# Attention on one NeuronCore: the row maxima are split into high and low part on 128 partitions and turned by VectorE in squares of 32, instead of by a TensorE matmul

## What is computed

```python
q = (x @ wq_w + wq_b).reshape(bs, sl, Q_H, HEAD_DIM)
k = (x @ wk_w + wk_b).reshape(bs, sl, KV_H, HEAD_DIM)
v = (x @ wv_w + wv_b).reshape(bs, sl, KV_H, HEAD_DIM)
qg = q.reshape(bs, sl, KV_H, FACTOR, HEAD_DIM)
scale = 1.0 / jnp.sqrt(jnp.asarray(HEAD_DIM, x.dtype))
attn = jnp.einsum('bqhfd,bkhd->bhfqk', qg, k) * scale
att = jax.nn.softmax(attn, axis=-1)
a = jnp.einsum('bhfqk,bkhd->bqhfd', att, v)
```

## Time and profile before

| | |
|---|---|
| median of three runs | 2863.34 us (2861.27 to 2865.27) |
| profiled execution | 2858.41 us, its span 2856.6 us |
| mean granted TensorE clock | 0.991 |
| TensorE busy | 2765.9 us |
| VectorE busy | 2196.1 us |
| GpSimd busy | 1914.0 us |
| ScalarE busy | 1519.8 us |

### The profile page before, as it was taken

The page is one execution under the profiler, slowest core; times in us unless marked ns, Lnnn a source line. Parts: engine busy times, 40 slices in busy tenths (PEclk is TensorE's granted clock), DMA queues, the critical chain, the costliest instruction groups (busy, mean ns, idle before and its releaser), DMA issues. The chain is left out here.

```text
span 2856.6 us, 48739 instructions
## 1 busy us (share of the span) xinstructions
PE 2765.9 (97%) x14654; PEld 1698.3 (59%) x14654; DVE 2196.1 (77%) x2775; ACT 1519.8 (53%) x2907; POOL 1914.0 (67%) x712
## 2 busy tenths in 40 slices
PE   7999999999999999999999999999999969999997
PEld 4788888874444444444444444444444427888886
DVE  4433343358999999999999999999999968666666
ACT  3111111117766666666666666667666733455444
POOL 2433333318999999999999999999999965111110
PEclk9999999999999999999999999999999989999998
DMA  7544444524444443343444334344433333333331
GB/s 268 178 141 140 140 136 143 151 91 123 95 96 89 87 99 83 86 98 85 90 94 95 89 86 94 89 89 90 99 86 85 71 108 114 111 102 97 111 110 67
DMA packets 167583, 307.60 MB, mean 108 GB/s; under 512 B 50000, under 2 KB 91408, under 8 KB 159376
## 3 DMA queue, kind: packets, MB, share of 16 engines
q1 hardware_dynamic: 158368, 240.05, 28.8%
q0 software_dynamic: 9072, 66.06, 11.3%
HBM read 159.12 MB, written 79.82 MB: 84 GB/s over the span
## 5 line engine op out<-in xcount | busy, mean ns | idle before, releaser
L1022 ACT ACTIVATE p_t<-st_ps 128x512 f32<-128x512 f32 x2048 | 1113.3, 596 | 465.2 <-PE st_ps L1140 393.4
L1040 DVE TENSOR_REDUCE mx<-s_ps 128x1 f32<-128x1024 f32 x1002 | 1172.9, 1209 | 109.3 <-PE s_ps L1114 100.0
L971 POOL TENSOR_TENSOR p_sum<-p_sum,p_t 128x2048 f32<-128x2048 f32 x254 | 1168.6, 4601 | 42.7 <-ACT p_t L1022 26.3
L1140 PE MATMUL st_ps<-q_st,k_st 98*128 98x512 f32 x2048 | 816.9, 438 | 21.4 <-ACT p_t L1022 19.0
L1140 PEld LDWEIGHTS st_ps<-q_st,k_st 98*128 98x128 f32 x2048 | 345.3, 187 | 615.8 <-ACT p_t L1022 515.5
L1114 PE MATMUL s_ps<-k_st,q_st 96*128 96x512 f32 x2004 | 629.9, 395 | 1.5 <-DVE mx L1040 1.3
L1154 PE MATMUL num_ps<-p_t,v_sb 128*32 128x512 f32 x4096 | 546.7, 606 | 0.9 <-ACT p_t L1022 0.9
L1114 PEld LDWEIGHTS s_ps<-k_st,q_st 96*128 96x128 f32 x2004 | 378.8, 189 | 73.4 <-DVE mx L1040 5.4
L1055 DVE TENSOR_REDUCE two_sum<-p_t 128x512 f32<-128x1024 f32 x256 | 317.4, 1241 | 3.1 <-DMA p_sum<-two_sum 3.1
L497 POOL TENSOR_TENSOR o_lo<-side,o_hi 128x512 fp32r<-128x512 f32 x80 | 104.2, 1303 | 321.3 <-ACT o_hi L467 321.1
L971 POOL TENSOR_TENSOR p_sum<-p_t 128x2048 f32<-128x2048 f32 x64 | 312.9, 4889 | 8.6 <-ACT p_t L1022 8.6
(11 more groups left out here) (141 smaller groups left out, 2884.8 us busy)
## 6 DMA issues: line engine op xcount, KB each, us to landing
p_sum<-two_sum POOLq DMA_DIRECT2D x63, 1024.0 KB, 7.0
q_st<-q_hi_d SPq DMA_DIRECT2D x128, 256.0 KB, 4.3
stage<-w_mod SPq DMA_DIRECT2D x48, 512.0 KB, 6.3
q_hi_d<-o_hi SPq DMA_DIRECT2D x64, 256.0 KB, 2.0
q_lo_d<-o_lo SPq DMA_DIRECT2D x64, 256.0 KB, 2.0
q_st<-q_lo_d SPq DMA_DIRECT2D x64, 256.0 KB, 4.1
att_d<-a_sb SPq DMA_DIRECT2D x128, 128.0 KB, 2.3
a_f<-att_d SPq DMA_DIRECT2D x32, 512.0 KB, 4.7
```

Of the source, the lines that this page charges most:

```text
L971: nc.gpsimd.tensor_tensor(total, before, p_t[:, kt, :, :], ALU.add).then_inc(sum_done, 1)
L1022: nc.scalar.activation(p_t[:, s, c, :], st_ps[:, c % 2, :], ACT.Exp, scale=SCALE)\
L1040: nc.vector.tensor_reduce(mx[:, slot % 2, e:e + 1], s_ps[:, e % 2, :], AX_X, ALU.max)\
L1140: nc.tensor.matmul(st_ps[:, c % 2, :], k_st[:, slot // 2, s * P:(s + 1) * P], q_st[:, slot, jj, h * QW:(h + 1) * QW], start=True, stop=True)\
```

## The change

The turn leaves TensorE. ScalarE now negates and rounds `mx` as it is, 128x16 from SBUF, into the left half of `m_parts`, and it does so behind the last exponential of step 4 (`NEGATE_STEP`). VectorE forms the rest into the right half at the beginning of step 5. Behind the `two_sum` of that step it turns `m_parts` in four squares of 32x32 (`m_t`) and copies the result into `m_rows`, which rounds it to fp32r. Each group of 32 partitions of `m_rows` then holds, for 32 queries of each of the 16 tiles, a row of 128 bytes for each part and tile, and SP places it by four transfers instead of two (`put_row`). `den_ps` no longer holds `m_ps`, so `add_sum` waits for `den_taken` alone, and `maximum` and `max_hi` keep their waits on `m_turned`, which VectorE now signals. The same is done once at the end of `project` for pair 0.

```diff
+def put_row(sp, q_st, slot, m_rows, landed):
+    rows = q_st[96:98, slot, :, :].bitcast(F32).rearrange("h j (t b r) -> h b (j t) r", b=4, r=32)
+    for b in range(4):
+        sp.dma_start(rows[:, b, :, :], m_rows[32 * b:32 * b + 32, :].bitcast(F32)).then_inc(landed, 16)
...
-    TURN_STEP = 5
+    NEGATE_STEP = 4
...
-        m_ps = den_ps[0:NS, 0:P]
...
                 def put_max(pair, slot):
-                    sp.wait_ge(m_lo_done, pair + 1)
-                    for n, part in enumerate((m_hi, m_lo)):
-                        sp.dma_start(q_st[STACK + n:STACK + n + 1, slot, :, :].bitcast(F32)
-                                     .rearrange("o j s -> o (j s)"), part[:, :].bitcast(F32))\
-                          .then_inc(m_in, 16)
+                    sp.wait_ge(m_ready, pair + 1)
+                    put_row(sp, q_st, slot, m_rows, m_in)
...
-                def max_hi(pair):
-                    act.wait_ge(m_turned, pair + 1)
-                    if not is_int(pair, 0):
-                        act.wait_ge(m_in, pair * 32)
-                    nc.scalar.activation(m_hi[:, :], m_ps, ACT.Copy, scale=-1.0).then_inc(m_hi_done, 1)
+                def max_hi(pair, slot):
+                    act.wait_ge(max_done, pair * NS + NS)
+                    act.wait_ge(m_turned, pair)
+                    nc.scalar.activation(m_parts[:, 0:NS], mx[:, slot % 2, :], ACT.Copy, scale=-1.0)\
+                      .then_inc(m_hi_done, 1)
...
-                            if c == 1 and s == TURN_STEP and not is_int(pair, NPAIR - 1):
-                                max_hi(pair + 1)
+                            if c == REP - 1 and s == NEGATE_STEP and not is_int(pair, NPAIR - 1):
+                                max_hi(pair + 1, (slot + 1) % QR)
...
-                def max_lo(pair):
+                def max_lo(pair, slot):
                     dve.wait_ge(m_hi_done, pair + 1)
-                    if not is_int(pair, 0):
-                        dve.wait_ge(m_in, pair * 32)
-                    nc.vector.scalar_tensor_tensor(m_lo[:, :], m_ps, -1.0, m_hi[:, :].bitcast(F32), ALU.mult,
-                                                   ALU.subtract).then_inc(m_lo_done, 1)
+                    nc.vector.scalar_tensor_tensor(m_parts[:, NS:2 * NS], mx[:, slot % 2, :], -1.0,
+                                                   m_parts[:, 0:NS].bitcast(F32), ALU.mult, ALU.subtract)\
+                      .then_inc(m_lo_done, 1)
+
+                def turn_max(pair):
+                    dve.wait_ge(m_lo_done, pair + 1)
+                    nc.vector.transpose(m_t[:, :], m_parts[:, :].bitcast(F32)).then_inc(m_turned, 1)
+                    dve.wait_ge(m_turned, pair + 1)
+                    dve.wait_ge(m_in, pair * 64)
+                    nc.vector.tensor_copy(m_rows[:, :], m_t[:, :]).then_inc(m_ready, 1)
...
-                        if s == TURN_STEP + 1 and not is_int(pair, NPAIR - 1):
-                            max_lo(pair + 1)
+                        if s == NEGATE_STEP + 1 and not is_int(pair, NPAIR - 1):
+                            max_lo(pair + 1, (slot + 1) % QR)
                         if s == 0 and not below(pair, 1):
                             add_two(pair - 1, REP - 1)
                         if s in TWO_STEPS:
                             add_two(pair, TWO_STEPS.index(s))
+                        if s == NEGATE_STEP + 1 and not is_int(pair, NPAIR - 1):
+                            turn_max(pair + 1)
...
-                    nc.tensor.matmul(m_ps, mx[:, slot % 2, :], ident[:, :], start=True, stop=True)\
-                      .then_inc(m_turned, 1)
...
-                        pe.wait_ge(m_in, pair * 32 + 32)
+                        pe.wait_ge(m_in, pair * 64 + 64)
...
-                        if is_int(pair, NPAIR - 2):
-                            pe.wait_ge(den_taken, NPAIR - 2)
-                        else:
-                            pe.wait_ge(m_lo_done, pair + 3)
+                        if not below(pair, 1):
+                            pe.wait_ge(den_taken, pair)
```

More of the change, by code:

```diff
@@ L31 @@
     mx: Any
-    m_hi: Any
-    m_lo: Any
+    m_parts: Any
+    m_t: Any
+    m_rows: Any
     s_ps: Any
@@ L39 @@
     m_turned: Any
+    m_ready: Any
     m_hi_done: Any
@@ L396, in do @@
                         elif ev[0] == "negate":
-                            sp.wait_ge(ahead.m_lo_done, 1)
-                            for n, part in enumerate((ahead.m_hi, ahead.m_lo)):
-                                sp.dma_start(ahead.q_st[3 * HD + n:3 * HD + n + 1, 0, :, :].bitcast(F32)
-                                             .rearrange("o j s -> o (j s)"), part[:, :].bitcast(F32))\
-                                  .then_inc(ahead.m_in, 16)
+                            sp.wait_ge(ahead.m_ready, 1)
+                            put_row(sp, ahead.q_st, 0, ahead.m_rows, ahead.m_in)
                         elif ev[0] == "rows":
@@ L817, in sem @@
             return ctx.enter_context(nc.semaphore(name))
-        q_st, k_st, mx, m_hi, m_lo, s_ps = ahead.q_st, ahead.k_st, ahead.mx, ahead.m_hi, ahead.m_lo, ahead.s_ps
+        q_st, k_st, mx, s_ps = ahead.q_st, ahead.k_st, ahead.mx, ahead.s_ps
+        m_parts, m_t, m_rows, m_ready = ahead.m_parts, ahead.m_t, ahead.m_rows, ahead.m_ready
         v_sb = sb("v_sb", [P, 2, NKT, HD], F32)
@@ L1199, in do @@
                             add_sum(pair - 1, (slot - 1) % 2)
-                        if s == TURN_STEP and not is_int(pair, NPAIR - 1):
-                            turn_max(pair + 1, (slot + 1) % QR)
                         scores(pair, slot, s, 2)
```

40 lines of the change are left out of this document (17 added, 23 removed).

## The result

The changed kernel takes 3283.48 us, the median of four runs (3280.34 to 3285.73); the kernel before took 2863.89 us beside it. The ratio is 1.1466, with a 95% interval from 1.1451 to 1.1481: 14.7% slower. The forecast was 3234 us, and its range ended at 3280, so the time lies 3.5 us outside the range. The profiled execution has a span of 3278.5 us, and the mean granted clock of TensorE is 0.929 against 0.991 before.

The account below looks back on a forecast made before the run. It took GpSimd to be as full as TensorE, both nearly unbroken. Per pair -0.20 + 4.68 (stall) + 1.5 (clock) = +5.98 us; 62 pairs add 371 to 2858.4, giving 3229, plus 4.9: 3234 us, range 3080 to 3280.

Parts of the forecast that it names:

- The race and the port: Step 5: VectorE's copy comes 0.1 to 0.2 us after a 4.6 us GpSimd sum begins, held to its end.
- The price of the hold: Step 6: TensorE waits for maxima delayed by VectorE's held copy, a stall of 4.68 us a pair.
- rival (a): Attention loop: VectorE's copy is held but TensorE's clock costs nothing; +4.48 us a pair, 3141 us; chance 11%.
- The clock: TensorE after the stall, step 7: 3.4 us at half clock, taken as 1.5 us a pair, bounds 0 to 1.7.
- the forecast alone: Main case, held copy plus low clock: 3165 us (clock 0.6 a pair) to 3270 (clock 1.7, hold 0.3 longer); chance 68%.
- The rest of the change: Attention loop: ScalarE's negating copy, SP's four transfers and the waits cost zero; the turn off TensorE saves 0.20 us a pair.
- GpSimd's ring: GpSimd's work from one join to the next in the attention loop, 25.97 us a pair, idle only 0.66.
- The net 0.23 us of VectorE: Steps 5 and 6: three new VectorE operations issue in 0.42 us, less 0.19 for the dropped `m_lo`.
- rival (c): Step 5: copy unheld, but VectorE's extra work and a held remainder cost 0 to +0.3 us a pair; 2863-2882 us; 7%.
- (b): Attention loop: copy held in only part of the pairs; half of them gives about 3050 us; chance 6%.
- (d): Step 5: copy goes before GpSimd's sum; not slower, 2860 us, or 2850 if GpSimd gave way; chance 8%.

Follow-up runs that it names:

- the run with the clock kept up: Changed kernel plus 16 unread matmuls on TensorE ahead of the first half entry of step 6, inside its wait: 3140.15 us, ratio 1.0973.
- the kernel of two reduces: Changed kernel with both VectorE's copy into `m_rows` and the remainder (`mx` less its rounded part) written as reduces: 2881.78 us, ratio 1.0069.

## Why the prediction came out as it did

**The race and the port: right.** The earlier trace rows gave GpSimd's sum at T5 + 1.70 and the sum of VectorE's steps the copy at T5 + 1.89; the rows after show + 1.78 and + 1.99. The copy was held to the end of the sum in all 62 pairs in which the prediction counted it. That it is the kind of instruction was only argued from the earlier trace rows; the reduce in its place, with 186 ns, shows it. That the GpSimd instruction sets the length is shown by three lengths: 4.37 us from its beginning, 2.38 from its middle, 2.2 with half a sum. The kernel with the copy ahead of the sum shows that the order of issue decides, as the prediction had it. The runs show which instructions exclude each other, and no run shows that a port is the reason. The Trainium skill ("SBUF — State Buffer", section "Who interferes with whom") names casts in a two-port mode and operations with two SBUF inputs on one side, reduces and ScalarE on the other; all four agree here (4365 and 1130 ns held, 186 and 218 not).

**The price of the hold: right.** 4.68 less 0.20 of turn makes 4.48 us a pair; the run with the clock kept up has 4.48 from the medians and 4.49 from the pairs. Its time, 3140 us, is what rival (a) gave with 3141. The parts fit too: the third half entry of step 6 was put at T5 + 8.82 and starts there at + 8.73 (1522.98 against 1514.25), and the numerators ahead of T5 take 1.00 us instead of 1.19 once the turn is gone (1509.68 to 1510.68 in the changed kernel). One detail was missing: the first half entry waits as well, for the first of the two held maxima, and TensorE's long idle time stands ahead of it, with little left ahead of the third. That cost an experiment and not the sum.

**The clock: the step that failed.** The sum had 1.5 us a pair, from 3.4 us at half clock behind one gap of the trace of before, and called 1.7 its upper bound. Measured are 2.31. The surplus of 0.81 us in 62 pairs is 50 us, which is the whole difference between 3234 and 3283.5. In its place stands: the low stretch lasts 6.8 us in most pairs, twice what that gap showed. Over the whole execution, (1 - 0.929) x 2 x 3278.5 = 466 us ran at the low clock against (1 - 0.991) x 2 x 2856.6 = 51 before, 6.7 us a pair. Half of that would be 3.35 us, and 2.31 were lost; part of the low time is idle (1.75 us in the pair shown above, next to none in the following one), and where the rest of the difference went no run shows. One gap was made a bound; the range ended at 3280 for that reason. The trace of before held more. It has a gap of 7.52 us with a low stretch of 6.8 us (0.30 us of the window 2323, six whole ones, 0.54 of the window 2330), and in the attention loop itself an idle time of 0.99 us with 3.4 us at 0.50 behind it:

```profile
2327.60 1.94 PE L1171 MATMUL den_ps<-p_sum,ones 128*32 128x512 f32 x8 [7.52 <-DVE den_t L1064]
...
1058.49 0.99 PE L1140 MATMUL st_ps<-q_st,k_st 98*128 98x512 f32 x2 [0.99 <-ACT p_t L1022]
```

```profile
2324.00:2325.00 1.00, 0.00 (x0) 0.00 (x0) 1.00 (x2) 0.00 (x0) 0.00 (x0) 0.50 0.00 0
...
1061.00:1062.00 1.00, 1.00 (x8) 0.13 (x8) 1.00 (x2) 0.63 (x2) 1.00 (x1) 0.50 0.24 49
```

The prediction's spread for the forecast alone was added up wrongly as well: by its own terms 2863.3 + 62 x (4.48 + 0.6) gives 3178 and not 3165, and a clock of 1.7 with a hold longer by 0.3 gives 3265 and not 3270. Neither would have taken in the result.

**The rest of the change: right.** Turn, negation, transfers, bank and waits were put at nothing beside GpSimd's ring, and the kernel without the copy is at 1.0006. ScalarE's copy, the transfers and the waits need no correction. The net 0.23 us of VectorE was hidden by the hold; where nothing is held, remainder and turn cost nothing (pairs of 25.96) and the third operation 0.27 a pair. That the kernel of two reduces measures 2881.78 us, the upper end of rival (c) with 2882, is luck in part: (c) counted a held remainder, and that kernel has none.

**The rivals.** (b) didn't occur: the copy came 0.18 to 0.31 us behind the sum's start in each pair, where GpSimd had waited for ScalarE and was thereby tied to T5. (d) was right that GpSimd's ring keeps the 0.20 us of TensorE from showing: with nothing held the pair stays at 25.96.

Not settled: why the remainder was kept out for 6.87 us through the ends of two GpSimd instructions in one pair; and what decides whether the clock falls behind an idle time of about 1 us, and whether its low stretch lasts 3.4 or 6.8 us. No run was made for either.

## What to carry to other kernels

Before a small VectorE copy, cast or two-input operation in SBUF is put into a stretch in which GpSimd works without a break, look which GpSimd instruction will be running when it is issued: its remaining length was the length of the hold in all pairs but one here, for an operation of 0.17 or 0.18 us. Write the small operation as a reduce, give it to ScalarE, or drop it, as here where the values were already rounded. To issue it just ahead of the long instruction is not safe: the copy ahead of the sum was still too late in five pairs of 63. And where a stall of TensorE recurs in a loop, count it with the low clock behind it, with the cost that runs show, and look at every low stretch of the trace, not at one gap.

## What the runs showed of the hardware that I had not expected

- Idle times of 3.70 and of 1.90 us in each pair cost the same 2.3 us of clock; with 1.54 us the clock fell in a part of the pairs, with 0.86 in three pairs of seven; with 0.40 us behind 3.81 us of filling work it never did, although every fourth pair there has 1.1 to 1.4 us of idle time besides. In the kernel before, such idle times of about 1 us stand in every fourth pair too, and the clock fell behind one of them. So the length of one idle time alone does not decide. The Trainium skill ("TensorE: Matmul & The Clock Gate", section "HAM oscillation — how this bites in real kernels") describes a kernel whose clock drops again at the wait of every tile; the traces agree with the repetition, 6.7 us at the low clock a pair in the mean, and they show it after shorter idle times than the one of the earlier trace rows.
- 3.81 us of useless matmuls in each pair made the kernel 4.4% faster.
- Issued 0.01 us ahead of GpSimd's sum the copy took 0.18 us (1466.02), issued 0.01 us behind it 4.56 (1854.67), in the same kernel.
- Taking away one hold brings out another: with GpSimd no longer idle, a two-input operation of 0.17 us that was free took 1.13 in every second pair.
